# A decoder layer on one core: the fold of the expert weights and the causal zeros move to GpSimd, with a new job table

## What is computed

```python
x = _layernorm(x + _L0_attn_ref(x, ...), axis=-1)
x = _layernorm(x + _L0_xattn_ref(x, ctx_512, ...), axis=-1)
x = _layernorm(x + _L0_ffn_ref(x, ...), axis=-1)
```

```python
for e in range(E):
    h = jnp.einsum('btd,hd->bth', x, W1[e]) + b1[e]
    a, b = jnp.split(h, 2, axis=-1)
    g = a * jax.nn.sigmoid(b)
    eo = jnp.einsum('bth,dh->btd', g, Wo) + bo
    out = out + eo * comb[..., e:e + 1]
```

## Time and profile before

| what | us |
|---|---|
| median of three runs (lowest, highest) | 189.89 (189.65, 189.92) |
| the profiled execution | 191.22 |
| its span, first to last instruction | 189.5 |
| TensorE busy within the span | 172.8 |
| VectorE busy | 148.8 |
| ScalarE busy | 114.7 |
| GpSimd busy | 40.6 |

### The profile page before, as it was taken

The page is one execution under the profiler, slowest core; times in us unless marked ns, Lnnn a source line. Parts: engine busy times, 40 slices in busy tenths (PEclk is TensorE's granted clock), DMA queues, the critical chain, the costliest instruction groups (busy, mean ns, idle before and its releaser), DMA issues.

```text
span 189.5 us, 5111 instructions
## 1 busy us (share of the span) xinstructions
PE 172.8 (91%) x2037; PEld 93.1 (49%) x2048; DVE 148.8 (79%) x324; ACT 114.7 (61%) x169; POOL 40.6 (21%) x147
## 2 busy tenths in 40 slices
PE   7998897999999989999699999999999999999970
PEld 3654352445342366645445654665667744444440
DVE  7489961697598769998959989959867459989994
ACT  3743299693949688568557671876589633442510
POOL 7165300014000113002100110103343440003224
PEclk9999999999999999999969999999999999999997
DMA  5990000000000000000000000000000000000001
GB/s 141 303 383 24 4 3 0 6 0 3 4 0 0 4 2 3 6 1 3 3 4 3 2 5 5 0 9 7 1 6 3 3 0 0 0 2 0 0 0 55
DMA packets 2984, 4.75 MB, mean 25 GB/s; under 512 B 753, under 2 KB 1489, under 8 KB 2961
## 3 DMA queue, kind: packets, MB, share of 16 engines
q1 hardware_dynamic: 2962, 4.44, 7.1%
HBM read 4.02 MB, written 0.26 MB: 23 GB/s over the span
## 4 chain that ended last, share of the span: by engine, by line
PE 68%; DVE 16%; ACT 9%; issue 4%; POOL 2%; POOLq 0%; DVEq 0%; ACTq 0%
PE t L718 14%; PE y L630 7%; ACT probs L1007 6%; DVE mneg L825 5%; PE t L376 5%; PE w L700 4%; PE t L532 4%; PE t L580 4%; PE y L595 3%; PE y L613 2%; PE t L571 2%; DVE mneg L838 2%; PE t L521 2%; PE t L566 2%; PE t L517 1%
## 5 line engine op out<-in xcount | busy, mean ns | idle before, releaser
L1007 ACT ACTIVATE probs<-t 128x1024 f32<-128x1024 f32 x60 | 58.6, 1028 | 7.5 <-PE t L580 3.3
L838 DVE TENSOR_REDUCE mneg<-t 128x2 f32<-128x1024 f32 x32 | 38.1, 1220 | 6.0 <-PE t L532 5.7
L718 PE MATMUL t<-w1T,x1T 128*128 128x512 f32 x64 | 29.2, 597 | 0.0
L1054 ACT ACTIVATE part_c<-t 128x512 f32<-128x512 f32 x16 | 9.6, 597 | 19.0 <-PE t L718 19.0
L825 DVE TENSOR_REDUCE mneg<-t 128x4 f32<-128x1024 f32 x16 | 18.9, 1217 | 2.5 <-PE t L499 2.4
L1126 POOL CAST mpart<-mneg 128x8 bf16<-128x8 f32 (+1 forms) x13 | 2.7, 208 | 81.4 <-DVE mneg L838 53.2
L630 PE MATMUL y<-probs,v_c 128*32 128x128 f32 x512 | 17.3, 276 | 0.0
L718 PEld LDWEIGHTS t<-w1T,x1T 128*128 128x128 f32 x64 | 11.5, 190 | 11.7 <-issue 11.4
L630 PEld LDWEIGHTS y<-probs,v_c 128*32 128x32 f32 x512 | 13.0, 109 | 2.5 <-issue 1.7
L832 DVE TENSOR_REDUCE mneg<-t 128x4 f32<-128x1024 f32 (+1 forms) x12 | 14.0, 1207 | 0.0
L1012 ACT ACTIVATE y_sb<-y 128x512 f32<-128x512 f32 x12 | 7.2, 602 | 8.7 <-PE y L613 5.4
(11 more groups left out here) (256 smaller groups left out, 300.7 us busy)
## 6 DMA issues: line engine op xcount, KB each, us to landing
w1T<-in_w1T SPq DMA_DIRECT2D x8, 256.0 KB, 8.0
rest<-in_rest SPq DMA_DIRECT2D x1, 772.0 KB, 7.7
bias_row<-in_rows SPq DMA_DIRECT2D x1, 384.0 KB, 6.4
ctx_room<-in_ctx SPq DMA_DIRECT2D x1, 320.0 KB, 5.7
first<-in_first SPq DMA_DIRECT2D x1, 262.5 KB, 2.8
q_stack_C<-mrow_C SPq DMA_DIRECT2D x16, 3.0 KB
out<-rest SPq DMA_DIRECT2D x4, 64.0 KB, 1.6
first<-in_first SPq DMA_DIRECT2D x1, 128.0 KB, 2.7
```

The costliest lines, as they stand in the source:

```text
L718: last = nc.tensor.matmul(o, x2T[:, (2 * b + q) * P:(2 * b + q + 1) * P], w1T[:, e, :], start=True, stop=True)
L838: emptied(V.tensor_reduce(out=dst, in_=o[:].rearrange("p (i k) -> p i k", i=2), axis=AX.X, op=ALU.max, negate=True), ("SC", b, q, p))
L1007: emptied(A.activation(probs[:, n % NPT, :], o[:], ACT.Exp, scale=SCALE), src)
L1054: A.activation(tanh_b[:, n % NTANH], o[:, :, HF:2 * HF], ACT.Tanh, scale=0.5).then_inc(s_tanh, 1)
```

## The change

The fold leaves TensorE. SP loads only the first 127 rows of each expert's weights (w), and besides, with a new job bw per expert, 127 copies of that expert's last row into spare room: the tile last_row for the first four, gT and two of the gated tiles for the others. b1 goes straight to partition 127 (bb, without a wait). GpSimd subtracts the copies from the weights (ws0 to ws7, each waits until both loads of the expert are there) and does the same with the gate (bg, wg). F waits for all eight ws. The mask_k matmuls are gone: the second pass of part B makes unmasked scores, and GpSimd sets the probabilities that the mask would have made zero to zero (zB, one affine_select for each of the twelve UB) before PB may read them. The idle matmuls are gone but for N6. The order of all lists is new. In it SP issues bg, bw0, bb, bw1 to bw7 and w0 to w7 ahead of mA00; GpSimd has ws0 and ws1 ahead of sA01 and all but ws5 ahead of sA10. The core of the diff:

```diff
...
     "pool": """
-        ib ov xr om sA00 bs ob sA01 sA10 rA0 xA0 sA11 sC000 sC001 rA1 xA1 sB01 sC011 sC100 sC101 sB11 sC110 rX01 sC111 rX00 gp01
-        rX10 gp00 gp10 rX11 gp11 rO00 rO01 rO10 rO11""",
+        ib ob ov xr om wg sA00 ws0 ws1 sA01 ws4 ws2 ws6 ws3 ws7 sA10 ws5 rA0 sA11 xA0 sC001 sB01 rA1 xA1 sC010 zB000 zB001 sC100
+        zB010 zB011 rX00 zB012 zB013 gp00 rX01 sC111 sC110 zB100 zB101 sB11 gp01 rX10 zB110 zB111 zB112 zB113 gp10 rO01 rX11
+        gp11 rO10 rO00 rO11""",
     "sp": """
-        w0 w1 w2 w3 w4 w5 w6 w7 mA00 mA01 mA10 mA11 mC000 mC001 mB00 mC010 mC011 mB01 mC100 mC101 mB10 mB11 bb mC110 mC111 st00
-        st10 st01 st11""",
+        bg bw0 bb bw1 bw2 bw3 bw4 bw5 bw6 bw7 w0 w1 w2 w3 w4 w5 w6 w7 mA00 mA01 mA10 mA11 mC001 mC000 mB01 mB00 mC010 mC011
+        mC101 mC100 mB10 mC111 mC110 mB11 st01 st10 st00 st11""",
 }
...
     "pe": """
-        N6:w0 JQA0:w0 JKA0:t0 JQA1:t1 JKA1:w0 RQA00:t0 RQA01:t2 DKA11 DQA11 RKA0:t2 N2:y SA00:t0 SA03:t2 DKA12 DQA12 SA06:t0
...
+        N6:w0 JKA0:w0 JKA1:t0 JQA0:t1 DKA11 RKA0:w0 JQA1:t1 DKA12 DQA11 RQA00:t2 RQA01:t0 DQA12 VA:w0 SA00:t2 RQA10:t1 RQA11:t0 VC1:w0
+        SA02:t2 SA03:t1 KC0:w0 SA01:t0 SA04:t1 DKC01 SA07:t2 SA06:t0 DKC02 TA00:t1 SA05:t0 RKA1:w0 RKC10:t1 RKC11:t2 KC1:w0
+        SA14:t0 SA12:t2 UA00:t1 DKC11 UA01:t0 TA01:t1 SA11:t2 SA13:t1 DKC12 SA10:t2 SA16:t0 UA02:t1 VC0:w0 UA03:t0 UA04:t1
...
@@ -237,6 +237,14 @@
         tanh_b = part_c[:].rearrange("p r n -> p (r n)").bitcast(F32).rearrange("p (r n h) -> p r n h", r=NTANH, n=2)
         gated_2 = sb("gated_2", [P, 2, 2, HF])
         gated = [gated_2[:, n] for n in range(2)] + [first[0][:, 0:2 * HF].rearrange("p (n h) -> p n h", n=2)]
+
+        def row_room(e):
+
+            if e < 4:
+                return last_row[:, e, :]
+            room = gT[0:P - 1, 2 * e - 8:2 * e - 6, :] if e < 6 else gated[e - 6][0:P - 1]
+            return room.rearrange("p n h -> p (n h)")
+
...
-                                nc.tensor.matmul(o[:, c0:c0 + P], k_stack_b[half(i, KROW), p, q0 + kt * P:q0 + (kt + 1) * P],
+                                last = nc.tensor.matmul(o[:, c0:c0 + P], k_stack_b[half(i, KROW), p, q0 + kt * P:q0 + (kt + 1) * P],
                                                  q_stack["B"][half(i, KROW), p, q0 + q * P:q0 + (q + 1) * P],
-                                                 start=(m == 0 and kt == 0), stop=False)
-                    for i in range(2):
-                        diag = o[:, i * 512:(i + 1) * 512].rearrange("p (m k) -> p m k", k=keys)[:, :, q * P:keys]
-                        last = nc.tensor.matmul(diag, ident_bf[:], mask_k[:, 0:len(pairs), :], start=False, stop=True)
+                                                 start=(m == 0 and kt == 0), stop=(m == len(pairs) - 1 and kt == q))
                     give(last, job)
...
-                    wait_emptied(pe, ("UB", b, q, n))
+                    pe.wait_ge(s_zeroed, nth[("zB", b, q, n)])
...
-                elif kind in ("WM", "WG"):
-                    if once("fold"):
-                        pe.wait_ge(s_fold, 1)
-                    if kind == "WG":
-                        if once("rest"):
-                            pe.wait_ge(ld_rest, 16)
-                        source = w_gT
-                    else:
-                        pe.wait_ge(ld_w1[b], 16)
-                        source = w1T[:, b, :]
-                    o = take(slot, job)
-                    give(nc.tensor.matmul(o[:, 0:E if kind == "WG" else 2 * HF], fold[:], source, start=True, stop=True), job)
                 elif kind == "GL":
                     _, b, q = job
-                    if once("WG"):
-                        wait_emptied(pe, ("WG",))
+                    if once("gate"):
+                        pe.wait_ge(s_gate_w, 1)
...
                     _, b, q, e = job
+                    if once("biases"):
+                        pe.wait_ge(s_b1, 16)
                     if once("experts"):
-                        pe.wait_ge(s_b1, 16)
+                        pe.wait_ge(s_less, E)
...
-                elif kind == "cWM":
-                    o = wait_full(dve, ("WM", b))
-                    emptied(V.tensor_copy(w1T[:, b, :], o[:, 0:2 * HF]), ("WM", b))
...
-                elif kind in ("cWM", "cWG"):
-                    src = ("WM", b) if kind == "cWM" else ("WG",)
-                    o = wait_full(act, src)
-                    dst = w1T[:, b, :] if kind == "cWM" else w_gT
-                    emptied(A.activation(dst, o[:, 0:E if kind == "cWG" else 2 * HF], ACT.Copy), src)
...
                 elif kind == "om":
-                    for t in (mask_q, mask_k):
-                        ins = G.memset(t[:], 0.0)
-                    link(ins)
+                    link(G.memset(mask_q[:], 0.0))
                     for n in range(4):
-                        G.affine_select(out=mask_q[:, n, :], in_=mask_q[:, n, :], compare_op=ALU.is_ge, fill=NEG, base=0,
-                                        pattern=[[-1, P]], channel_multiplier=1)
-                        ins = G.affine_select(out=mask_k[:, n, :], in_=mask_k[:, n, :], compare_op=ALU.is_ge, fill=NEG, base=0,
-                                              pattern=[[1, P]], channel_multiplier=-1)
+                        ins = G.affine_select(out=mask_q[:, n, :], in_=mask_q[:, n, :], compare_op=ALU.is_ge, fill=NEG, base=0,
+                                              pattern=[[-1, P]], channel_multiplier=1)
                     ins.then_inc(s_mask, 1)
...
-                elif kind == "bs":
-                    link(G.memset(fold[:], 0.0))
-                    link(G.affine_select(out=fold[:], in_=fold[:], compare_op=ALU.not_equal, fill=1.0, base=0,
-                                         pattern=[[-1, P]], channel_multiplier=1))
-                    link(G.affine_select(out=fold[:], in_=fold[:], compare_op=ALU.is_ge, fill=-1.0, base=P - 2,
-                                         pattern=[[0, P]], channel_multiplier=-1))
-                    G.affine_select(out=fold[:], in_=fold[:], compare_op=ALU.is_ge, fill=0.0, base=P - 2,
-                                    pattern=[[-1, P]], channel_multiplier=0).then_inc(s_fold, 1)
+                elif kind == "ws":
+                    pool.wait_ge(ld_w1[b], 32)
+                    G.tensor_tensor(w1T[0:P - 1, b, :], w1T[0:P - 1, b, :], row_room(b), ALU.subtract).then_inc(s_less, 1)
+                elif kind == "wg":
+                    pool.wait_ge(ld_rest, 16)
+                    pool.wait_ge(ld_gate, 16)
+                    G.tensor_tensor(w_gT, w_gT, gate_row[:], ALU.subtract).then_inc(s_gate_w, 1)
+                elif kind == "zB":
+                    _, b, q, n = job
+                    wait_emptied(pool, ("UB", b, q, n))
+                    keys = (q + 1) * P
+                    diag = probs[:, unit_of[("EB", b, q, n)] % NPT, :].rearrange("p (m k) -> p m k", k=keys)[:, :, q * P:keys]
+                    G.affine_select(out=diag, in_=diag, compare_op=ALU.is_ge, fill=0.0, base=0,
+                                    pattern=[[0, 1024 // keys], [1, P]], channel_multiplier=-1).then_inc(s_zeroed, 1)
...
                 elif kind == "w":
-                    sp.dma_start(w1T[:, b, :], packs["w1T"][:, b * 2 * HF:(b + 1) * 2 * HF]).then_inc(ld_w1[b], 16)
+                    sp.dma_start(w1T[0:P - 1, b, :], packs["w1T"][0:P - 1, b * 2 * HF:(b + 1) * 2 * HF]).then_inc(ld_w1[b], 16)
+                elif kind == "bw":
+                    sp.dma_start(row_room(b),
+                                 packs["w1T"][P - 1, b * 2 * HF:(b + 1) * 2 * HF].partition_broadcast(P - 1)).then_inc(ld_w1[b], 16)
+                elif kind == "bg":
+                    cols = packs["rest"].shape[1]
+                    sp.dma_start(gate_row[:], packs["rest"][P - 1, cols - E:cols].partition_broadcast(P)).then_inc(ld_gate, 16)
                 elif kind == "bb":
-                    for e in range(E):
-                        wait_emptied(sp, ("WM", e))
                     sp.dma_start(w1T[P - 1:P, :, :].rearrange("p e n -> p (e n)"), packs["b1"]).then_inc(s_b1, 16)
...
```

More of the change, by code:

```diff
@@ L39 @@
     "pe": """
-        N6:w0 JQA0:w0 JKA0:t0 JQA1:t1 JKA1:w0 RQA00:t0 RQA01:t2 DKA11 DQA11 RKA0:t2 N2:y SA00:t0 SA03:t2 DKA12 DQA12 SA06:t0
-        RKA1:w0 RQA10:t1 RQA11:t2 N1:y SA02:t0 VA:w0 SA01:t1 N1:y SA04:t0 SA05:t2 N1:y SA07:t1 N2:y SA12:t2 N2:y TA00:t0 KC0:w0
-        SA13:t0 SA11:t1 DKC01 TA01:t2 N1:y UA00:t0 UA01:t2 DKC02 UA02:t0 UA03:t1 SA10:t2 VC0:w0 UA04:t0 UA05:t2 UA06:t1 PA000
-        TA10:w0 UA07:t0 PA001 RKC00:t2 RKC10:t1 RKC11:t0 PA010 PA011 RKC01:t0 YA01:w0 YA00:t1 UA10:t2 SA15:t0 SA17:t1 ZA0:w0
@@ L44 @@
[L44 to L60, removed]
@@ new lines @@
+        SA02:t2 SA03:t1 KC0:w0 SA01:t0 SA04:t1 DKC01 SA07:t2 SA06:t0 DKC02 TA00:t1 SA05:t0 RKA1:w0 RKC10:t1 RKC11:t2 KC1:w0
+        SA14:t0 SA12:t2 UA00:t1 DKC11 UA01:t0 TA01:t1 SA11:t2 SA13:t1 DKC12 SA10:t2 SA16:t0 UA02:t1 VC0:w0 UA03:t0 UA04:t1
```

(23 more changed lines are left out.)

42 lines of the change are left out of this document (21 added, 21 removed).

## The result

The changed kernel takes **346.83 us** (median of four runs, 346.57 to 347.13) against 189.89 us: 1.827 times as long, 95% interval 1.8238 to 1.8302. Forecast were 333 us and the range 313 to 350. The profiled execution took 346.68 us for a span of 344.9.

What follows compares the result with a forecast made beforehand. The prediction took one DMA engine working off all 127-row loads as the bound: UA00 at 181.7 us plus 151.2 us behind it gave 332.9 us of span, so 333 us (chance 0.74), range 313 to 350.

Steps and rivals of the forecast that it cites:

- the stall and its cause: Weight loads ahead of UA00: all 127-row loads line up on one DMA engine until 180.7 us, UA00 at about 181.7.
- the rival of spread loads: Weight loads: 127 rows spread over 16 engines, or each load on another engine; 178 us, chance 0.10.
- SP's nine added issues at 0.4 to 0.6 us each end at about 13.5 us, before 20.48: nothing.: SP queue ahead of mA00: issuing the added loads ends before mA00's old issue time, so costs nothing.
- GpSimd's gate alone: Rival: one engine for all loads, but none of mA00's three; UA00 on time, sA10 waits; 327 us, chance 0.10.
- GpSimd's gate: GpSimd's queue: ws jobs wait for loads ahead of sA01 and sA10, so sA10 can't start before near 182 us.
- zB, forecast at 1.2 and 0.7 us: GpSimd between exp and PB: affine_select on 1,024 or 512 elements, taken as hidden (0); uncovered 10.4 us, at most 17.6.
- the stretch behind UA00: From UA00 to the end: 165.6 us before, forecast 151.2 after deletions, moved work and restart.
- So I add 1 us (0 to 2): TensorE after the stall: cost of restarting at the 1.2 GHz clock, mostly hidden by ScalarE's exp.
- What was taken off: Behind UA00: fold 8.3 us, mask_k 3.8, idle pieces 1.3, and 2 for KC1 and VC1 moved ahead.
- the order eats the gain: Rival behind UA00: stall as forecast, new order's waits (zB, ws, late sA10) cancel the deletions; 347 us, chance 0.06.
- The close of the sum: Last step: 332.9 us of span became 333, the median of runs being taken as 0.4 us above the span.
- the 145 to 160 that the prediction gave as its sign: Sign of being right: the stretch from UA00 to the end lasts 145 to 160 us, without L700 and L571.

Runs made afterwards that it cites:

- Experiments 1 to 3: experiment 1, experiment 3 and, between them, the changed kernel with each of its 16 loads cut in 124 rows and 3 rows: 222.84 us in one execution.
- experiment 4: The changed kernel (127 rows) with all ws jobs moved behind xA0 in GpSimd's list: 350.04 us in one execution.
- experiment 6: The changed kernel plus 36 idle matmuls ahead of UA00, four groups of four between UA00 and UA04, and twelve later: 341.95 us.
- experiment 8: The changed kernel with 128-row loads (experiment 1) plus twelve idle matmuls where TensorE had waited: 186.14 us, ratio 0.9784 to the kernel before.
- experiment 3: The kernel before with only its eight w loads each cut in 127 rows and 1 row: 262.46 us in one execution.
- experiment 7: The kernel before without its 26 later idle matmuls, N6 kept: 197.18 us, ratio 1.0355.
- experiment 1: The changed kernel with every w and bw load moving 128 rows, the bias load behind mA11: median 196.48 us of six executions.

## Why the prediction was right and where it was wrong

**Right: the stall and its cause.** 127 rows go to one engine (one ending a load, 25 GB/s), and mA00's share stands behind them. UA00 came at 178.1 us, forecast 181.7. Of the 3.6 us, 16 x (10.67 - 10.46) = 3.4 are the row's price, 82 ns against the 84 worked out from the earlier trace rows. Experiments 1 to 3 leave no room for the rival of spread loads.

**Wrong: "SP's nine added issues at 0.4 to 0.6 us each end at about 13.5 us, before 20.48: nothing."** They end at 158.4 us. An issue was held for 10.42 us while the one engine worked off its line; with 128 rows it was not. This is a third gate that the prediction didn't have. It shows no cost of its own, for mA00 waits for the same engine anyway and UA00 came no later than forecast. Had mA00 needed none of its share there, the rival "GpSimd's gate alone" would still have put UA00 too early, as mA00's issue began only at 158.4 us; this is worked out, no run tries it.

**Right, but not decisive: GpSimd's gate.** ws takes 1.26 us (forecast 1.25), and sA01 stood behind ws1. GpSimd was through with ws7 at 179.0 us and sA10 waited for VectorE until 188.9; experiment 4 shows that moving ws gains nothing. zB, forecast at 1.2 and 0.7 us, shows in the instructions of the kernel after on tile probs:

```profile
L1110 POOL TENSOR_SCALAR_AFFINE_SELECT probs<-probs x12: 634/663/1275, 247.9 to 305.8; 128x512 f32<-128x512 f32 x8, 128x1024 f32<-128x1024 f32 x4
```

The quick slope of the earlier trace rows was the right one. That zB was hidden, as forecast, wasn't tried by itself; no wait for it stands among TensorE's largest.

**Wrong in size: the stretch behind UA00, 166.8 us, not 151.2.** Two terms failed.

*"So I add 1 us (0 to 2)" for the restart.* The row it rested on was one dip of 3.4 us. TensorE restarted at 1.2 GHz and stayed there for 15.8 us, busy for 15.3 of them, and shorter dips followed. With the clock held the stretch is 161.6 us behind the same stall (experiment 6) and 158.8 without a stall (experiment 8): between 5 and 8 us. The restart alone cost less: in experiment 3, the old order with its later idle matmuls, UA00 to the end took 260.7 - 93.0 = 167.7 us, 2.0 more than in the profiled execution of before and 3.3 more than in one at its median, though the granted clock stood at 0.50 from 92.9 to 100 us there too (one execution). The deletion of the idle matmuls had been costed at a gain, as idle pieces on the chain (1.3 us); experiment 7 shows that they were worth 7.3 us to the kernel before. The prediction quoted the Trainium skill (TensorE: Matmul & The Clock Gate, Part 1) against taking them out, and the runs agree with the direction; the sum gave it 1 us.

*What was taken off: the fold's share of the chain, 8.3 us, mask_k's, 3.8, idle matmuls, 1.3, and 2 moved ahead.* TensorE's busy time did fall by 14.5 of these 15.4 us, but 7.7 came back as waits (experiment 8). A share of the chain was taken for a gain. A reading that fits: the fold matmuls needed nothing that VectorE or ScalarE were just making, so they filled TensorE's time while VectorE's maxima were late, and with them gone it waits for the maxima. It would account for the 4.5 us more on mneg, not for the 2.4 more in the tail, where the kernel before has the idle matmuls N5 instead. It is not shown: no run takes out the fold alone, and the order is new too. So the rival "the order eats the gain" (347 us, 0.06) comes nearest in microseconds, and of its waits those for zB and ws are not the ones that show: about half the gain went into waits for VectorE above all, the rest to the restart and the lower clock behind it. The two terms make up the miss: 8.0 - 1 for the restart, 15.4 - 14.5 for the busy time and 7.7 for the waits are 15.6 us.

*The close of the sum:* the execution was put 0.4 us above its span, by setting the median of some executions beside the span of another; each execution took 1.7 to 1.9 us more than its own span. The median is 346.83 - 344.9 = 1.9 above. In all -3.6 + 15.6 + 1.5 = 13.5 us over the unrounded 333.3. That the time lies within 313 to 350 is earned by the stall, which was forecast by its mechanism. For the stretch behind it, it is in part luck: 166.8 us lies outside the 145 to 160 that the prediction gave as its sign, and the range reached up to it only because it took in a rival that was held unlikely.

What stays open: the idle matmuls of experiment 6 took back 5.2 of the 8.0 us. Whether the other 2.8 (161.6 against 158.8) are work piled up behind the stall is not shown, for these sixteen more idle matmuls behind UA00 are themselves TensorE time, 140.9 us busy against 137.6. And why four executions of experiment 1 were at clocks near 0.89 and two near 0.95 is not settled; with the idle matmuls (experiment 8) six executions lay within 0.6%.
